# Linear attention and a routed block on one core: start-up order, weight copies and last norms moved

## The reference

```python
xn = layernorm(x)                                    # x: 2048 tokens x 512, float32
# first half: linear attention with decay, 16 heads of 32, in blocks
q, k, v, u = split(xn @ W_qkvu.T); q, k = silu(q), silu(k)
o = (q_i * q_decay) @ kv + ((q_i @ k_i.T) * diag_decay) @ v_i
kv = block_decay * kv + (k_i * k_decay).T @ v_i      # state carried over blocks
attn = (u * o * rsqrt(mean(o * o) + eps)) @ W_out.T
# second half: the 256 tokens with the highest router score
scores = xn @ w_router; idx = sorted(top_k(scores, 256)); s = xn[idx]
h = rms_norm(s, ln1); q, kk, v = rope(h @ wq + bq), rope(h @ wk + bk), h @ wv + bv
x1 = s + causal_softmax(q @ kk.T / sqrt(128)) @ v @ wo    # 16 heads, 8 key heads of 128
h2 = rms_norm(x1, ln2)
p = x1 + (silu(h2 @ w_gate) * (h2 @ w_up)) @ w_down
out = x + attn + xn.at[idx].set(g * p + (1 - g) * s)      # g = sigmoid(score)
```

## Time and profile before

| | us |
|---|---|
| median of 3 runs | 487.58 |
| lowest, highest | 487.25, 488.27 |
| the profiled execution | 489.89 |
| its span, first to last instruction | 488.2 |

### The profile page before, as it was taken

One profiled execution on the slowest core, in us unless ns is written; L12 is line 12 of the kernel. 1 busy time (PEld: TensorE's weight loads), 2 busy tenths in 40 slices (PEclk: granted clock), 3 DMA queues, 4 the chain that ended last, 5 costly groups with the idle time before them and its releaser, 6 DMA issues. The chain is left out here.

```text
span 488.2 us, 11974 instructions
## 1 busy us (share of the span) xinstructions
PE 471.3 (97%) x4887; PEld 427.5 (88%) x4887; DVE 292.6 (60%) x611; ACT 230.5 (47%) x404; POOL 189.1 (39%) x179
## 2 busy tenths in 40 slices
PE   7998999999999999999999998999999989999994
PEld 6998899898998999987989877889888878999993
DVE  5889666864288978652457687886764436230221
ACT  7921232221267677321262447664765866454420
POOL 3012251111101232014149669431462441789862
PEclk9999999999999999999999999999999999999999
DMA  7943244112310111005525436655446352555503
GB/s 235 378 143 126 70 132 130 54 58 88 131 43 25 28 44 44 3 23 175 191 90 179 133 139 222 217 179 186 147 158 216 125 178 88 150 173 176 170 1 43
DMA packets 32886, 62.15 MB, mean 127 GB/s; under 512 B 3440, under 2 KB 3456, under 8 KB 32704
## 3 DMA queue, kind: packets, MB, share of 16 engines
q1 hardware_dynamic: 32288, 60.08, 36.6%
q0 software_dynamic: 544, 1.31, 1.4%
HBM read 48.27 MB, written 13.12 MB: 126 GB/s over the span
## 5 line engine op out<-in xcount | busy, mean ns | idle before, releaser
L1141 POOL TENSOR_TENSOR wlo<-raw,whi 128x512 fp32r<-128x512 f32 x96 | 125.9, 1343 | 83.6 <-ACT whi L535 83.6
L1207 PE MATMUL banks<-HTh,whi 128*128 128x256 f32 x224 | 64.8, 289 | 2.8 <-DVE rope L885 2.7
L1208 PE MATMUL banks<-HTl,whi 128*128 128x256 f32 x224 | 63.3, 283 | 0.0
L1209 PE MATMUL banks<-HTh,wlo 128*128 128x256 f32 x224 | 63.3, 283 | 0.0
L805 DVE TENSOR_TENSOR A<-banks,DEC 128x512 f32<-128x512 f32 x64 | 39.8, 684 | 36.0 <-PE banks L1271 34.8
L1120 POOL TENSOR_TENSOR state_dec<-state,small 128x128 f32<-128x128 f32 x16 | 8.5, 529 | 113.1 <-DVE state L816 113.1
L535 ACT ACTIVATE whi<-raw 128x2048 fp32r<-128x2048 f32 x24 | 45.8, 1908 | 10.1 <-PE banks L1209 10.1
L1207 PEld LDWEIGHTS banks<-HTh,whi 128*128 128x128 f32 x224 | 42.8, 191 | 4.5 <-issue 4.1
L1208 PEld LDWEIGHTS banks<-HTl,whi 128*128 128x128 f32 x224 | 42.9, 191 | 0.2
L1209 PEld LDWEIGHTS banks<-HTh,wlo 128*128 128x128 f32 x224 | 42.9, 191 | 0.0
L1253 PE MATMUL banks<-xTh,WKh 128*128 128x256 f32 x128 | 37.9, 296 | 0.8 <-DVE xTl L738 0.8
(11 more groups left out here) (235 smaller groups left out, 1301.7 us busy)
## 6 DMA issues: line engine op xcount, KB each, us to landing
X<-in_x SPq DMA_DIRECT2D x16, 256.0 KB, 3.6
xn_all<-XN SPq DMA_DIRECT2D x16, 256.0 KB, 2.7
uo_all<-uo SPq DMA_DIRECT2D x16, 256.0 KB, 2.7
raw<-in_wq SPq DMA_DIRECT2D x4, 1024.0 KB, 5.2
UR<-uo_all SPq DMA_DIRECT2D x16, 256.0 KB, 5.3
XR<-in_x SPq DMA_DIRECT2D x16, 256.0 KB, 3.2
raw<-in_wo SPq DMA_DIRECT2D x4, 1024.0 KB, 5.7
out<-XR SPq DMA_DIRECT2D x16, 256.0 KB, 2.1
```

The source lines that it names most:

```text
L1141: ins = Q.tensor_tensor(low[:, k, :], raw[b % 3][:, k, :], high[:, k, :].bitcast(f32), ALU.subtract)
L1207: T.matmul(dst, lh, rh, start=first, stop=False)
L1208: T.matmul(dst, lh, rl, start=False, stop=False)
L1209: return T.matmul(dst, ll, rh, start=False, stop=last)
```

## The change

It has five parts.

- The load of token tile 1 and the two small loads of decay rates (shead, shid) go from SP's queue to ACT's, ahead of its first instruction. SP issues token tile 0, then the key weights at once.
- On ACT, part 1 of the decay tables goes from ahead of the key weights to behind the query weights, and the value weights' high parts go from the first loop pass to between part 1 and part 2. On DVE the statistics of token tiles 2 and 3 go behind the low query weights.
- PE does projection tile 0 in another order: high weights by high input for both halves of its columns and all four k, then high weights by low input, then low weights by high input, with a wait for each where it is first needed. The other tiles stay as they are.
- Block Q2 is copied and made low in step 1 instead of 0, block U0 in step 18 instead of 16, and block D0 is loaded in step 19 instead of 17. From step 12 on the copy stands behind OTh of the same step, not ahead of it.
- The two PN operations of heads 14 and 15 are done by DVE, behind the reciprocal, instead of ACT.

```diff
--- before.py
+++ after.py
@@ -205,8 +205,8 @@
 
             return u + 1 - kq_count(u)
 
-        hi_after = {0: "Q2", 2: "O0", 4: "Q3", 6: "O1", 8: "O2", 9: "O3", 12: "G0", 16: "U0"}
-        load_at = {0: "Q3", 1: "O1", 3: "O2", 5: "O3", 7: "G0", 9: "U0", 10: "G1", 13: "U1", 17: "D0"}
+        hi_after = {1: "Q2", 2: "O0", 4: "Q3", 6: "O1", 8: "O2", 9: "O3", 12: "G0", 18: "U0"}
+        load_at = {0: "Q3", 1: "O1", 3: "O2", 5: "O3", 7: "G0", 9: "U0", 10: "G1", 13: "U1", 19: "D0"}
 
         def ln_tiles(N):
             return [M for M in (2 * N + 7, 2 * N + 8) if NXN <= M < N_TILES]
@@ -383,9 +383,6 @@
                 sp.dma_start(raw[b % 3][:], source[k[0]](int(k[1]))).then_inc(raw_in[b % 3], 16)
 
             load_x(0)
-            sp.dma_start(shead, s_head.partition_broadcast(P)).then_inc(shead_in, 16)
-            load_x(1)
-            sp.dma_start(shid, s_hid).then_inc(shid_in, 16)
             for k in range(NK):
                 sp.dma_start(raw_w["K"][:, k, :], WT_v[:, k, DM:2 * DM]).then_inc(w_raw_k[k], 16)
             load_x(2)
@@ -565,15 +562,19 @@
                     evacuate(tiles[position])
                 elif u is not None and units[u][0][0] == "V":
                     unit_values(u)
+            act.dma_start(X[:, 1, :], x_t[1]).then_inc(x_in[1], 16)
+            act.dma_start(shead, s_head.partition_broadcast(P)).then_inc(shead_in, 16)
+            act.dma_start(shid, s_hid).then_inc(shid_in, 16)
             act.wait_ge(consts, 1)
             S.activation(table_dump[:, 0:1], eps_rms, ACT.Exp)
             decay_tables(0)
-            decay_tables(1)
             first_weights_hi("K", w_raw_k, k_w_hi, (0, 1))
             xt_high(0)
             xt_high(1)
             first_weights_hi("K", w_raw_k, k_w_hi, (2, 3))
             first_weights_hi("Q", w_raw_q, q_w_hi, range(NK))
+            decay_tables(1)
+            weights_hi("V", v_w_hi)
             decay_tables(2)
             S.activation(table_dump[:, 1:2], eps_rms, ACT.Silu)
             for N in slots_of_chunks:
@@ -582,8 +583,6 @@
                     block_hi(0)
                 in_position(N, 0, tiles)
                 count_marks(ranked(N, 0))
-                if N == -2:
-                    weights_hi("V", v_w_hi)
                 in_position(N, 1, tiles)
                 if N >= 1:
                     mean_square(N - 1)
@@ -655,17 +654,19 @@
                     if p >= 2:
                         act.wait_ge(ot_ps, p - 1)
                     S.activation(PT[:, p % 2, :], B[4][:, 0:3 * P], ACT.Copy).then_inc(pt_ok, 1)
-                if h < FH:
+                if h < FH - 2:
                     normalised(h)
                 if h in out_at:
                     base(out_at[h])
-                if h in hi_after:
+                if h in hi_after and h < late_outs[0] - 1:
                     block_hi(block_of[hi_after[h]])
                 if 0 <= g < FH:
                     act.wait_ge(ot_ps, g + 1)
                     if g >= 2:
                         act.wait_ge(wo_ps, g - 1)
                     S.activation(OTh[:, g % 2, :], B[5][:, 0:SEL], ACT.Identity, bias=value_bias(g)).then_inc(ot_hi, 1)
+                if h in hi_after and h >= late_outs[0] - 1:
+                    block_hi(block_of[hi_after[h]])
             act.wait_ge(var_s_ok, 2)
             act.wait_ge(gate_ok, 1)
             for t in range(NS):
@@ -925,9 +926,9 @@
             for M in range(CH):
                 xt_low(M)
             first_weights_lo("K", k_w_hi, k_w_lo, (1, 2, 3))
+            first_weights_lo("Q", q_w_hi, q_w_lo)
             for M in range(CH, NXN):
                 ln_stats(M)
-            first_weights_lo("Q", q_w_hi, q_w_lo)
             for M in range(CH, NXN):
                 ln_norm(M)
             first_weights_lo("V", v_w_hi, v_w_lo)
@@ -1012,6 +1013,12 @@
                     if h >= 2:
                         dve.wait_ge(pn_ok, h - 1)
                     V.reciprocal(pinv[:, h % 2, :], psum_[:, h % 2, :]).then_inc(sum_ok, 1)
+                if FH - 2 <= h < FH:
+                    dve.wait_ge(sum_ok, h + 1), dve.wait_ge(pt_ps, h - 1)
+                    for t, cols in ((0, slice(0, P)), (1, slice(P, 3 * P))):
+                        ins = V.tensor_scalar(PN[:, h % 2, cols], PR[:, h % 2, cols], pinv[:, h % 2, t:t + 1], None,
+                                              ALU.mult)
+                    ins.then_inc(pn_ok, 1)
                 if h in unit_of_step:
                     stage(unit_of_step[h])
                 if h in out_at:
@@ -1229,13 +1236,26 @@
                 g, i = tile // NPROJ, tile % NPROJ
                 name, j = "KQVU"[i // 2], i % 2
                 w_split = W_SPLIT[name]
-                if i == 0:
+                if i == 0 and g:
                     pe.wait_ge(xt_lo, CH * (g + 1))
                 if g == 0 and j == 0 and name in "VU":
                     pe.wait_ge(v_w_lo if name == "V" else u_w_lo, NK)
                 if tile >= 4:
                     pe.wait_ge(proj_sb, tile - 3 if tile < 6 else tile - 1)
                 bank = proj_bank(tile)
+                if tile == 0:
+                    pe.wait_ge(xt_hi, CH)
+                    for n, (w, xt) in enumerate(((w_split[0], xTh), (w_split[0], xTl), (w_split[1], xTh))):
+                        for k, half in ((k, half) for k in range(NK) for half in range(2)):
+                            if half == 0 and n != 1:
+                                pe.wait_ge(k_w_lo if n else k_w_hi, k + 1)
+                            if n == 1 and k == half == 0:
+                                pe.wait_ge(xt_lo, CH)
+                            ins = T.matmul(bank[:, half * GROUP:(half + 1) * GROUP], w[:, k, half * P:(half + 1) * P],
+                                           xt[:, 0, k, :], start=n == k == half == 0, stop=n == 2 and k == NK - 1,
+                                           skip_group_check=True)
+                    ins.then_inc(proj_ps, 1)
+                    return
                 steps = 3 * NK
                 for step in range(steps):
                     if name == "V":
```

## The result

| | before | after |
|---|---|---|
| median, us | 487.41 (4 runs) | 494.56 (4 runs) |
| lowest, highest | 486.76, 488.27 | 493.41, 496.00 |
| the profiled execution, its span | 489.89, 488.2 | 496.0, 494.3 |

The ratio is 1.0144, 95% interval 1.0116 to 1.0172. The change makes the kernel 7.1 us slower; the forecast was 2.45 us slower, and its range ended at 493.0. The direction was right and the size was not. Three later executions took 1163 us; no ratio uses them, nor does the median given for `halves_and_middle_2`.

The account below looks back on a forecast made before the run. PE, busy 471.3 of 488.2 us, was taken to bound the kernel. Terms of +1.5 (start), +0.65 (middle) and +0.3 (tail) sum to +2.45 over the 487.58 median, giving 490.0 us; range 487.7 to 493.0.

Parts of the forecast that it names:

- PE's first matmul at 10.4: Start of projection tile 0: PE begins at about 10.4 instead of 11.38, 1.0 us earlier.
- The early gain ends at kdec: PE's lead of 1.0 to 1.8 us stops at 44.70, where it waits for chunk 0's decayed keys.
- Start +1.5: First stage: ACT's xTh of tile 2, and kdec with it, come 1.5 us later; ends 0.96 and 1.97.
- The upper end, 16.44 + 7.01: First stage: value weights land at 16.44 as now, ACT's 7.01 us follow, xTh at 23.45, 1.97 us later.
- the 0.45 us taken off for an earlier landing: First stage: value weights assumed to land 0.45 us earlier, as SP issues weight loads about 1.4 us earlier.
- the queue buys nothing: Rival on the second load queue: first stage costs +1.97 instead of +1.5, total 490.5 us; chance 0.17.
- The clock: Rival: a wait of some 4 us at 44.70 drops PE's clock, costing some 2.8 us, total 493.0; chance 0.12.
- Middle +0.65 (0 to +1.9): Q2's copy a step later: PE gains 1.2 us at 304.02, but O1's and UR's loads slip 1.9; net +0.65.
- the 1.25 us that I took off its top: Middle: 0.5 us off +1.9 for a shorter landing, 0.75 us for uol falling behind GpSimd's block.
- Tail +0.3 (-0.1 to +0.9): Last norms on DVE, U0 later: two waits go, but U0's low part delays the last transposes; net +0.3 us.
- the 1.29 us: Tail: PE's waits of 0.38 and 0.91 us before the last attention products both go, a gain of 1.29.
- Range: Whole kernel: 487.7 to 493.0 us, widened from 488.4 to 492.3 by part of the no-change and clock cases.

Follow-up runs that it names:

- halves_and_middle_2: Kernel before with PE's new order of tile 0, Q2's copy at step 1 and O1's load at step 2, second run: 488.82 us, ratio 0.9978.
- halves_alone: Kernel before with only PE's order of projection tile 0 changed: 486.49 us, ratio 0.9985.
- s1_first_stage: Kernel before with only the first-stage changes (two load queues, key weights ahead of decay tables, new tile 0 order): 490.62 us, ratio 1.0057.
- s1_one_queue: Kernel before with the first-stage changes, but the three moved loads back on SP's queue: 491.03 us, ratio 1.0068.
- tables_back: Kernel before with first-stage changes, but the three loads on SP's queue and decay tables part 1 ahead of the key weights again: 493.57 us, ratio 1.0065.
- tail_root_first: Kernel before with only the tail changes, plus GpSimd's power operation for the last norm ahead of U0's low part: 489.78 us, ratio 1.0048.
- after_filled: Changed kernel with 16 unused identity matmuls added ahead of the transposes of tile 4, where PE waits: 493.13 us, ratio 1.0109 against the kernel before.

## Why the prediction was right or wrong, step by step

- **PE's first matmul at 10.4**: 10.78. The 0.64 us that xTh was to gain did not come; it started 0.25 us later than before, because s_head, moved to the second queue, held the first tables to 6.87. I had counted the three issues as a gain for SP and looked at no landing but V's.
- **The early gain ends at kdec**: right. kdec ended at 46.59, just past the window of 45.5 to 46.5, and PE idled 4.11 us, in the middle of the forecast 3.5 to 4.5. It holds for the changed kernel, where ACT is the later of the two; with PE's order alone the gain passed (`halves_alone`, -0.72).
- **Start +1.5**: +2.0 against the profiled execution of before, +1.90 to +2.46 against the second in four traces. The upper end, 16.44 + 7.01, gave +1.97 and was the right arithmetic: V landed at 16.57. The step that failed is the 0.45 us taken off for an earlier landing: V was issued at 7.67 against 7.64, so the 1.4 us that SP gained never reached it. The rival "the queue buys nothing" was true in this term.
- **The clock**, at nothing in the forecast's sum: the rival happened, behind this wait of 3.9 to 4.1 us in all five traces that kept it (two of the changed kernel, `s1_first_stage`, `s1_one_queue`, `tables_back`), and cost 1.4 to 2.6 us each time; filling the wait removed it. A second fall, behind the last transposes, cost 1.2 us more and was in no rival. I gave 0.12 because no pause of that length could be read. The trace behind the forecast did not show that the clock also falls in half of the runs of the kernel before. The rule of the Trainium skill named there (TensorE: Matmul & The Clock Gate, HAM oscillation) agrees with the granted clock of 0.50 behind the 4.11 us.
- **Middle +0.65 (0 to +1.9)**: mechanism right in each link: wait at step 1 0.27, O1's load later, UR behind it, PE's wait two units on. Measured +0.96 to +1.09 in three traces, 1.9 to 2.3 in three others once the low clock is taken off. The term was undersized, by 0.3 us in the first three; in the others nothing was left of the 1.25 us that I took off its top for a shorter landing and for uol. A wait of 1.02 us before unit 10, at 313.22, was not forecast.
- **Tail +0.3 (-0.1 to +0.9)**: +1.87, outside its ends. The forecast chain is there link by link: last OTh, U0's copy, low part, power operation, delta, transposes. But it was wrong in three terms. Of the 1.29 us only 0.86 were gained, as one wait of 0.40 stayed. From the end of the last OTh to the transposes it took 9.61 us instead of 9.06, with a low part of 5.94 us beside DVE for my 5.47. And I read the shift at the transposes, 409.5 against 409.26, where PE did not wait before; DVE's delta ended at 408.56 before, and what DVE does behind it has no such slack, which cost 0.65 us more. 0.24 + 0.43 + 0.55 + 0.65 = 1.87. I also took DVE's statistics at their undisturbed 0.69 us. They doubled and more; they ended with GpSimd's block at 406.0, so here they added nothing to its chain, but a block beside DVE costs on either side, which is why the order on GpSimd alone won nothing (`tail_root_first`). The sign was in the prediction itself: uol at 1.75 us beside GpSimd; I applied it to the moved norms and not to what else DVE does beside the moved block.
- **The sum**: 2.45 against 5.0 at full clock (start 2.5, middle 1.1, tail 1.8 in `after_filled`, 5.4 together in the trace) and 7.1 in the median. Half of the miss is three undersized terms; start and tail lay beyond the worse of their ends, the middle in most traces between them. The rest is the clock. Each of the three terms had its sign right, so the direction was not luck.
- **Range**: it took in part of the clock case on top of the forecast, not on top of the high ends, though the same long wait makes both.

## What to carry to other kernels

Before work is moved away from the head of a list, ask what the engine would do there instead: a table that fills the landing of a load is free, and V's weights ahead of such a table turned 2 us of filler into idle time. A block load that waits for a buffer holds every transfer behind it; the moved copy paid only when that load went behind the small one. A block of GpSimd work is placed against all that DVE does in its time, not only against GpSimd's own list. A wait that a change lengthens on PE is priced with its length and with the clock behind it, here 1.2 to 2.6 us more.
